# Transposed x loaded from DRAM for the first channel mix, second buffers for retention, and a new order of work in a three-stage transformer block

## What is computed

```python
x = x + 0.5 * ffn(layernorm(x), W_r, W_k, W_v, mu_r, mu_k)
x = x + retention(layernorm(x), Wq, Wk, Wv) @ Wo     # 8 heads of 32
x = x + 0.5 * ffn(layernorm(x), W_r, W_k, W_v, mu_r, mu_k)

def ffn(x, ...):
    x_prev = x shifted by one token, the first is 0
    xr, xk = mu_r * x + (1 - mu_r) * x_prev, mu_k * x + (1 - mu_k) * x_prev
    return sigmoid(xr @ W_r.T) * (relu(xk @ W_k.T)**2 @ W_v.T)
```

## Time and profile before

| | us |
|---|---|
| Median of three runs | 339.44 (339.43 to 340.46) |
| The profiled execution, whole | 338.8 |
| Its span, first to last instruction | 336.9 |
| TensorE busy | 322.3 (96%) |
| VectorE busy | 297.0 (88%) |
| ScalarE busy | 210.5 (62%) |
| GpSimd busy | 135.1 (40%) |
| Share of TensorE in the chain that ended last | 88% |
| Transferred | 12.08 MB |

### The profile page before, as it was taken

How to read it: one execution, slowest core, us unless ns; L and a number is a source line. 1 busy time by engine, 2 the same in 40 slices (tenths; PEclk the granted TensorE clock), 3 DMA queues, 4 the chain that set the end, 5 groups by cost and what they waited for, 6 DMA issues and landing times.

```text
span 336.9 us, 11291 instructions
## 1 busy us (share of the span) xinstructions
PE 322.3 (96%) x4260; PEld 302.4 (90%) x4260; DVE 297.0 (88%) x696; ACT 210.5 (62%) x422; POOL 135.1 (40%) x242
## 2 busy tenths in 40 slices
PE   4979999999999999999999999999999999999975
PEld 4869899999999999999899999989999998989874
DVE  4989899999999999899999989999897979888954
ACT  2877556775757586674758567475857555374362
POOL 4386165608163451706245270715424154221130
PEclk9999999999999999999999999999999999999999
DMA  7610010102001020201102020100000010000001
GB/s 232 247 35 31 4 34 0 34 5 62 4 2 63 2 65 3 65 2 27 41 3 64 2 63 2 53 16 32 2 19 17 2 35 7 26 4 31 34 2 62
DMA packets 11556, 12.08 MB, mean 36 GB/s; under 512 B 1008, under 2 KB 11120, under 8 KB 11504
## 3 DMA queue, kind: packets, MB, share of 16 engines
q1 hardware_dynamic: 11072, 11.18, 10.4%
q10 hardware_dynamic: 432, 0.20, 0.2%
HBM read 7.18 MB, written 4.19 MB: 34 GB/s over the span
## 4 chain that ended last, share of the span: by engine, by line
PE 88%; DVE 4%; issue 3%; ACT 2%; POOL 1%; DMA 1%; ACTq 0%; DVEq 0%; POOLq 0%
PE psum L964 39%; PE psum L956 24%; PE psum L948 7%; PE psum L1035 5%; PE psum L1067 5%; PE psum L1054 3%; PE psum L1025 2%; PE psum L1080 2%; PE psum L1157 1%; DMA ident<-in_ident 1%; ACT xn L344 1%; DVE stats L624 1%; PE psum L1161 1%; PE psum L1127 1%; PE psum L1115 0%
## 5 line engine op out<-in xcount | busy, mean ns | idle before, releaser
L199 POOL TENSOR_TENSOR xr_lo<-xrT,xr_hi 128x512 fp32r<-128x512 f32 x24 | 41.1, 1728 | 99.8 <-ACT xr_hi L375 99.8
L344 ACT ACTIVATE xn<-x,shift,rstd 128x256 f32<-128x256 f32 x96 | 52.0, 591 | 10.1 <-POOL shift L283 10.1
L692 DVE TENSOR_TENSOR attn<-psum,decay 128x512 f32<-128x512 f32 x64 | 42.4, 683 | 4.7 <-PE psum L1035 4.7
L964 PE MATMUL psum<-w_hi,xr_hi 128*128 128x256 f32 x124 | 38.6, 312 | 1.7 <-DVE xr_lo L199 1.2
L624 DVE BATCH_NORM_STATS2 stats<-x 128x6 f32<-128x256 f32 x96 | 35.7, 414 | 4.9 <-DMA x<-in_x 4.6
L276 POOL TENSOR_TENSOR var_eps<-moments,eps 128x2 f32<-128x2 f32 x48 | 18.9, 395 | 43.7 <-DVE moments L628 42.9
L964 PE MATMUL psum<-w_hi,ka_hi 128*128 128x256 f32 x120 | 35.7, 297 | 0.7 <-ACT rgate L403 0.7
L956 PE MATMUL psum<-xa_hi,w_hi 128*128 128x256 f32 x128 | 35.8, 280 | 0.0
L956 PE MATMUL psum<-xk_hi,w_hi 128*128 128x256 f32 x120 | 34.5, 288 | 1.1 <-POOL xk_lo L193 0.9
L956 PE MATMUL psum<-xa_lo,w_hi 128*128 128x256 f32 x128 | 35.5, 278 | 0.0
L956 PE MATMUL psum<-xa_hi,w_lo 128*128 128x256 f32 x128 | 35.5, 277 | 0.0
(11 more groups left out here) (105 smaller groups left out, 1043.4 us busy)
## 6 DMA issues: line engine op xcount, KB each, us to landing
x<-in_x SPq DMA_DIRECT2D x15, 256.0 KB, 2.9
x_out<-y SPq DMA_DIRECT2D x15, 256.0 KB, 3.1
w_f<-in_w SPq DMA_DIRECT2D x7, 256.0 KB, 5.9
decay<-in_decay SPq DMA_DIRECT2D x1, 512.0 KB, 6.6
decq<-in_decq SPq DMA_DIRECT2D x1, 256.0 KB, 6.1
deck<-in_deck SPq DMA_DIRECT2D x1, 256.0 KB, 6.2
x_out<-y SPq DMA_DIRECT2D x2, 128.0 KB, 1.8
x<-in_x ACTq DMA_DIRECT2D x1, 128.0 KB, 2.8
```

What stands on the lines that cost most here:

```text
L199: engine.tensor_tensor(xr_lo[f][n % 2][:], xrT[f][n % 2][:], xr_hi[f][n % 2][:].bitcast(F32), ALU.subtract).then_inc(xr_lo_ready[f], 1)
L344: act.activation(xn[s][n % 2][:, t, :], x[n % len(x)][:, t, :], ACT.Identity, bias=shift[s][n % 2][:, t:t + 1], scale=rstd[s][n % 2][:, t: ...
L692: dve.tensor_tensor(attn[r][:], bank[B_SCORES[r]].rearrange("p (g c i) -> p g c i", g=G, c=TILES), decay[:, r, :, :].unsqueeze(2).broadcas ...
L964: mm = pe.matmul(halves(b)[:, t, :], xt[:, g, cols], wt[:, g, :], start=(j == 0), stop=(j == 5))
```

## The change

- From DRAM the kernel also reads a transposed copy of x, xT, which the host makes. For blocks 2 to 15 (FIRST_ROWS = 2) of FFN1 there is no normalize, no transpose_T, no evacuate_T and no halo. GpSimd still computes rstd and shift, now side by side in scale_shift. SyncE stores both as rows of 256 elements to DRAM (norm_rows, elements of 4 bytes) and loads them back to all 128 partitions, with one token more on the left. GpSimd computes xT * rstd (scale_xT) and adds shift (shift_xT), 128x514 each, straight into xnT.
- For these blocks ScalarE computes mu * xnT (scale_k, scale_r, two instructions of 128x256 each) and VectorE mixes (1 - mu) * xnT_prev + that; the difference falls away. mu_rest = 1 - mu is computed on GpSimd ahead of its first inverse_std, after a wait for mu.
- Three normalisations (FFN1 block 0, RET block 0, FFN2 block 15) are made on VectorE from mean and rstd (normalize_fast), with var_eps on VectorE too; only the power is left on GpSimd.
- qT, vrow, krow and state_dec get two buffers, x1 three. x0 keeps four. To make room two of the four attn buffers lie in the float32 weights of Wq and Wk.
- Warm-up multiplies a tile of zeros set by GpSimd (12 and 7 matmuls), and no longer waits for the identity.
- All lists are new. In TensorE's loop outer and intra stand one behind the other and inter comes later. VectorE's loop runs from 8 to 15 and ends with add_ffn(FFN1, i-3), xa_low(i-4). The banks of PSUM are dealt out anew.

```diff
-        x1 = ring("x1", 2, [TILES, D])
+        x1 = ring("x1", 3, [TILES, D])
...
+            def load_xT(n):
+                k = n - FIRST_ROWS
+                sp.wait_ge(xT_scaled, k)
+                sp.dma_start(xT[0][:], xT_groups[:, :, n * BT - 1:(n + 1) * BT]).then_inc(xT_loaded[0], 16)
+
+            def store_rows(n):
+                sp.wait_ge(shift_ready[FFN1], shifts(FFN1, n + 1))
+                for k in range(2):
+                    sp.dma_start(rows_out[k, n], scale_shift[FFN1][n % 2][:, k, :], allow_slow_non_contiguous=True).then_inc(rows_stored[n % 2], 16)
+
+            def load_rows(n):
+
+                k = n - FIRST_ROWS
+                sp.wait_ge(rows_stored[(n - 1) % 2], 32 * stored_rows(n - 1))
+                sp.wait_ge(rows_stored[n % 2], 32 * stored_rows(n))
+                sp.wait_ge(xnT_ready[FFN1], FIRST_ROWS + k if k > 0 else 0)
+                sp.dma_start(rows[0][:], rows_io[:, n * BT - 1:(n + 1) * BT].partition_broadcast(P)).then_inc(rows_loaded[0], 16)
...
+            for i in range(8, 16):
+                load_xT(i - 1)
+                load_rows(i - 1)
+                load_x(i)
+                store_rows(i)
+                store_y(i - 8)
...
+            def scale_xT(n):
+                k = n - FIRST_ROWS
+                pool.wait_ge(xT_loaded[0], 16 * (k + 1))
+                pool.wait_ge(rows_loaded[0], 16 * (k + 1))
...
+                pool.tensor_tensor(xnT[FFN1][n % 2][:], xT[0][:], rows[0][:, 0, :].unsqueeze(1).broadcast_to([P, G, BT + 1]),
+                                   ALU.mult).then_inc(xT_scaled, 1)
...
+            pool.wait_ge(mu_loaded, 16)
+            pool.tensor_scalar(mu_rest[:], mu[:], -1.0, 1.0, ALU.mult, ALU.add).then_inc(mu_rest_set, 1)
...
+            for i in range(9, 16):
+                xr_low(pool, FFN1, i - 4)
+                xr_low(pool, FFN2, i - 8)
+                inverse_std(RET, i - 5)
+                inverse_std(FFN2, i - 7)
+                scale_xT(i - 2)
+                shift_xT(i - 2)
                 inverse_std(FFN1, i)
...
+            for i in range(8, 16):
                 layer_stats(FFN1, i, x0)
...
+                update_state(0, i - 6)
+                difference(FFN2, i - 7)
+                scale_state(1, i - 6)
+                mix_r(FFN1, i - 3)
+                mix_k(FFN2, i - 7)
+                mix_r(FFN2, i - 7)
+                mix_k(FFN1, i - 2)
+                xk_low(dve, FFN2, i - 7)
+                o_low(i - 6)
+                gate(FFN2, i - 8)
+                decayed_query(i - 5)
+                add_ffn(dve, FFN2, i - 8)
+                update_state(1, i - 6)
+                layer_stats(RET, i - 4, x1)
+                add_retention(i - 6)
+                square_low(dve, FFN1, i - 3)
+                layer_stats(FFN2, i - 6, x2)
+                xk_low(dve, FFN1, i - 2)
+                scale_state(0, i - 5)
+                mask_scores(0, i - 5)
+                mask_scores(3, i - 5)
+                mask_scores(2, i - 5)
+                mask_scores(1, i - 5)
+                gate(FFN1, i - 3)
+                decayed_key(i - 5)
+                square_low(dve, FFN2, i - 7)
+                add_ffn(dve, FFN1, i - 3)
+                xa_low(i - 4)
...
+            add_ffn(dve, FFN1, 0, part=0)
+            add_ffn(dve, FFN1, 0, part=1)
+            layer_stats(FFN1, 4, x0)
             layer_stats(RET, 0, x1)
...
             for i in range(6, 16):
...
+                hidden(FFN1, i - 1, 1)
...
                 ffn_out(FFN2, i - 6, 0)
...
                 key(i - 3, 0)
...
+                inter(i - 4)
...
+                hidden(FFN1, i, 0)
+                pe.wait_ge(val_ready, i - 2)
+                outer(i - 3)
+                pe.wait_ge(gated[FFN1], i)
+                pe.wait_ge(krow_ready, i - 2)
+                intra(i - 3, first=True)
```

More of the change, by code:

```diff
@@ L182, in span, with shifts, stored_rows @@
             return slice(0, G) if part is None else slice(part, part + 1)
+        FAST = {(FFN1, 0), (RET, 0), (FFN2, 15)}
+        def shifts(s, n):
+            return sum((s, k) not in FAST for k in range(n))
+        def stored_rows(n):
+            return max((n - (FIRST_ROWS - 1)) // 2 + 1, 0)
         def splits(f, n):
@@ new lines, in _ @@
+            xr_low(pool, FFN1, 12)
+            xr_low(pool, FFN2, 8)
+            inverse_std(RET, 11)
+            inverse_std(FFN2, 9)
+            scale_xT(14)
+            shift_xT(14)
+            xr_low(pool, FFN1, 13)
+            xr_low(pool, FFN2, 9)
+            inverse_std(RET, 12)
+            inverse_std(FFN2, 10)
+            scale_xT(15)
+            shift_xT(15)
+            xr_low(pool, FFN1, 14)
+            xr_low(pool, FFN2, 10)
+            inverse_std(RET, 13)
+            inverse_std(FFN2, 11)
@@ L800, in _ @@
+            add_retention(1)
+            square_low(dve, FFN1, 4)
+            layer_stats(FFN2, 1, x2)
+            xk_low(dve, FFN1, 5)
+            scale_state(0, 2)
+            mask_scores(0, 2)
+            mask_scores(3, 2)
+            mask_scores(2, 2)
+            mask_scores(1, 2)
+            gate(FFN1, 4)
             decayed_key(2)
-            for i in range(6, 16):
+            square_low(dve, FFN2, 0)
+            add_ffn(dve, FFN1, 4)
+            xa_low(3)
+            for i in range(8, 16):
@@ new lines, in _ @@
+                gate(FFN1, i - 3)
[3 more added lines that the diff above has]
+                xa_low(i - 4)
+            update_state(0, 10)
+            difference(FFN2, 9)
+            scale_state(1, 10)
+            mix_r(FFN1, 13)
+            mix_k(FFN2, 9)
+            mix_r(FFN2, 9)
+            mix_k(FFN1, 14)
+            xk_low(dve, FFN2, 9)
+            o_low(10)
+            gate(FFN2, 8)
+            decayed_query(11)
@@ new lines, in _ @@
+            add_ffn(dve, FFN2, 8)
+            update_state(1, 10)
+            layer_stats(RET, 12, x1)
+            add_retention(10)
+            square_low(dve, FFN1, 13)
+            layer_stats(FFN2, 10, x2)
+            xk_low(dve, FFN1, 14)
+            scale_state(0, 11)
+            mask_scores(0, 11)
+            mask_scores(3, 11)
+            mask_scores(2, 11)
+            mask_scores(1, 11)
+            gate(FFN1, 13)
+            decayed_key(11)
+            square_low(dve, FFN2, 9)
@@ new lines, in _ @@
+            add_ffn(dve, FFN1, 13)
+            xa_low(12)
+            update_state(0, 11)
+            difference(FFN2, 10)
+            scale_state(1, 11)
+            mix_r(FFN1, 14)
+            mix_k(FFN2, 10)
+            mix_r(FFN2, 10)
+            mix_k(FFN1, 15)
+            xk_low(dve, FFN2, 10)
+            o_low(11)
+            gate(FFN2, 9)
+            decayed_query(12)
+            add_ffn(dve, FFN2, 9)
+            update_state(1, 11)
+            layer_stats(RET, 13, x1)
+            add_retention(11)
@@ L832, in _ @@
+            square_low(dve, FFN1, 14)
+            layer_stats(FFN2, 11, x2)
+            xk_low(dve, FFN1, 15)
+            scale_state(0, 12)
+            mask_scores(0, 12)
+            mask_scores(3, 12)
+            mask_scores(2, 12)
+            mask_scores(1, 12)
+            gate(FFN1, 14)
+            decayed_key(12)
             square_low(dve, FFN2, 10)
-            mask_scores(1, 12)
-            mask_scores(2, 12)
+            add_ffn(dve, FFN1, 14)
+            xa_low(13)
             update_state(0, 12)
-            mask_scores(3, 12)
+            difference(FFN2, 11)
@@ L928, in _ @@
             xk_low(dve, FFN2, 15, part=0)
+            xr_low(dve, FFN2, 15)
             gate(FFN2, 14)
[L930 to L931 removed]
+            square(dve, FFN2, 15, part=0)
             square_low(dve, FFN2, 15, part=0)
```

1137 lines of the change are left out of this document (583 added, 554 removed).

## The result

The changed kernel took 522.12 us (median; 521.15 to 524.64), the kernel before on the same chip 339.94 us (339.43 to 340.46): a ratio of 1.540 with a 95% interval of 1.535 to 1.544. The forecast was 348.0 us, from 337 to 357. The direction was right and the size was not: 182 us were added where 8 were forecast. The profiled execution has a span of 519.3 us against 336.9.

The account below looks back on a forecast made before the run. TensorE bounds the kernel at 19.40 us a block; after the change, the loop through x0 at 20.0. 338.8 + 7.0 (start) + 1.0 (middle) + 1.1 (end) = 347.9, said as 348 us, range 337 to 357.

Parts of the forecast that it names:

- The transposes, 0.44 us a block: TensorE, blocks 2 to 15: four transposes and a switch back fall away, period 19.40 to 18.96 us, 6.2 us in all.
- any of these prices is covered in the loop: SyncE's queue: four more transfers per block cost nothing in the loop, as rows are stored about 38 us before use.
- The closed loop through x0: Loop: statistics, addition, x request and landing form a chain through four buffers, 20.0 us a block, seven times.
- rival 3: SyncE's queue: the rows' load ahead of x holds it about 0.8 us; 354, up to 357 us; chance 0.05.
- rival 2: SBUF: VectorE and GpSimd operations with two SBUF inputs wait for each other, 0.85 us per period; 354 us; chance 0.10.
- the prediction's sum of 19.8: Loop through x0: 16.3 statistics to addition, 0.69 addition, 2.7 issue and landing, 0.1 semaphores; 20.0 us was then taken.
- GpSimd's two operations at 1.3 us: GpSimd, each block: two 128x514 operations with two SBUF inputs at 1.3 us each, bounds 1.3 and 1.8.
- VectorE at 17.5 us a block: VectorE, each block: loses one difference of 0.60 us, so its work falls from 18.1 to 17.5 us.
- The start, +7.0: Start: scores of block 3 at 90.3 us instead of 83.25, bounds +2 and +11; TensorE recovers about 5 of 12.0 us.
- Term (a): Start: GpSimd's first wait is for mu, at 7.05 us; first transposes near 9.3 instead of 7.90, 1.4 us late.
- Terms (b) to (e): Start: VectorE's extra work and its statistics waiting for x or additions cost 0.7, 3.1, 2.3 and 4.5 us.
- Middle and end: Scores of block 3 to 14: +1.0 us; from there to the end: +0.4 and +0.7, together +1.1 us.

Follow-up runs that it names:

- before_with_store: The kernel before, plus two unread stores of rstd and shift per block in 4-byte elements to a scratch tensor: 444.46 us.
- no_row_store: The changed kernel without the row stores and all waits for them, loading constants as rows: 378.19 us.
- no_store_five_x: The changed kernel without row stores (constant rows), with x requested ahead of xT and rows and a fifth x0 buffer: 345.29 us.
- one_store: The kernel before, plus the two unread 4-byte-element stores of block 8 only: 347.21 us.
- store_unwaited: The changed kernel with its stores sent to an unread scratch and constant rows loaded without waiting for them: 483.12 us.

## Why the prediction was wrong, by its own steps

**The transposes, 0.44 us a block: right in kind, 0.34 in size.** The changed kernel has 136 transposes of xn and not 192. In the stretches where TensorE is the bound, a block takes 19.04 to 19.06 us instead of 19.40. The forecast was 18.96.

**SyncE's four extra transfers, "any of these prices is covered in the loop": the step that failed.** The prediction itself noted that the trace has no 4-byte transfer. It then took prices from the nearest rows, a 2 KB load and loads of 256 KB, and put nothing behind them but the time until the data is needed. Two things were wrong with that. The landing is 17 to 20 us and not 2.5 to 5.8. Against that the cover is one iteration and not the two (38 us) that the prediction counts: the load of the rows stands one iteration behind the store, and SyncE, which issues in order, can't ask for x before it. And cover until the data is needed is no cover for the others that share the DMA engines: with nobody reading what was stored, and 2.7 us of waiting for it in all, the stores still cost 104 us (before_with_store), 7.4 us a block, because other transfers and, as argued above, instructions stand behind them. In the loop of the changed kernel they make 30.84 - 23.31 = 7.5 us a block, seven times. The larger part, 79.1 us, is at the start (176.5 against 97.3 at block 3), where the landing is on the path: the load of the first rows waits 15.3 us for the stores, and x of block 4, asked for behind it at 32.72 us, keeps VectorE waiting for 26.3 and, through the low part of W_R behind it, TensorE for 29.3. A further 11.1 us fall between the scores of blocks 10 and 15. Together 142.9 of the 182.4.

**The closed loop through x0: right, 20.0 a block forecast, 23.3 seen without the stores.** It is the same chain, and a fifth buffer removes it. The landing was 4.8 and not 2.8, and the 2.0 go when x is asked for ahead of xT and the rows: in kind rival 3, which I gave 0.05 and 0.8 us. No run moved the rows alone. The path from statistics to addition was 18.3 and not 16.3, by two instructions held by GpSimd: rival 2, which I gave 0.10 and 0.85 us a period. Neither takes the other's place; they add. With both the prediction's sum of 19.8 would have been 19.8 + 2.0 + 2.0 = 23.8, the iteration shown; the mean is 23.3. Treating them as rivals, each instead of the forecast, was the mistake: they are further terms of the same chain.

**GpSimd's two operations at 1.3 us: right,** 1.28 and 1.19 (medians of 14 each). **VectorE at 17.5 us a block:** 18.32 busy in the period shown, with the locked instruction in it.

**The start, +7.0: 14.2 without the stores.** Term (a) was wrong in sign. First transposes came at 7.55 us, earlier than the 7.90 before, and not at 9.3: in the changed kernel mu had landed by 5.8, not at 7.05. Terms (b) to (e) were too small. They were priced as delays of VectorE, while TensorE's longest wait there was for the low part of a weight (6.6 us in no_row_store; 5.2 and 3.3 in no_store_five_x), whose place in the lists of VectorE and GpSimd the prediction followed only for W_R. How the 14.2 us divide among the terms no run shows.

**Middle and end: right.** The last five blocks take 88.2 us without the stores, the sum of the forecast's own terms (3 x 18.96 + 16.1 + 15.2 = 88.2), and what lies behind the last scores grew by 0.7, as forecast.

**The range** had no term for the stores beyond what was called covered. The bound was taken from rows of another kind of transfer (few and large packets, reads), and the prediction never asked what a transfer does to those that it is not needed by.

## To carry to other kernels

Look at where each packet of a store lands, not only at its bytes: gather scattered 4-byte elements in SBUF first, and write DRAM in whole rows. When all engines are empty at once and the profile says "issue", suspect the DMA engines that also bring the instructions, and test it by adding the suspected transfer, unread, to a kernel that doesn't need it. Count how far apart a store and its load stand in the issuing engine's own list, and not when the data is used. In an in-order ring of buffers, add up every step from freeing to use as one loop; a lock and a transfer ahead in the queue are terms of that sum and not alternatives to it.

## What the runs showed of the hardware

- 512 writes of 4 bytes into neighbouring places of DRAM cost 7.57 us at one blow: issued at 120.61 and 121.13 us in one_store, they leave all engines idle from 128.2 to 133.3 us. The same packets 64 or 512 bytes apart cost nothing (338.8 and 339.9 us), and in SBUF nothing (340.5). The Trainium skill (DMA: Bandwidth & Descriptors, section "Back-pressure in remote DMA") says, of writes to another core, that stalled writes stall the DMA engine's other queues too; no run here has writes to another core, but an instruction packet of another queue that took 4.9 and 10.6 us instead of 0.9 fits it.
- The share of the DMA engines does not tell such a stall: it is 0.00 in the windows of one_store and before_with_store where everything stands, but 0.98 in store_unwaited from 89 to 92 us, where everything stands too. Queue q1 went from 10.4% to 13.7% only in before_with_store. What shows it is the longest time to landing (of x 8.0 us in before_with_store and 15.7 in store_unwaited, where both medians stay at 2.8), and engines that are empty at once, at "issue" or "remote".
- TensorE's granted clock was 0.50 in the windows that follow a stand of some 5 us in which it did nothing, where a 128x256 matmul steps on by 0.21 us and not by 0.12; over the whole span it was 0.85 in the changed kernel and 0.999 before.
- Two rows of VectorE instructions with two SBUF inputs, met near their start by a GpSimd subtraction, took 1.03 us longer each.
